# A graph network of four residual layers on one core: three tiles of source rows fetched by one-hot products instead of indirect DMA

## What is computed

```python
# layer 2 (src, dst and etypes have 400,000 entries)
h_src = feat[src]
for r in range(16):
    mask = etypes == r
    msg = msg + h_src * mask[:, None].astype(feat.dtype) @ weight[r]
out = jax.ops.segment_sum(msg, dst, num_segments=feat.shape[0])
# layer 3
m = jnp.concatenate([x[row], x[col], edge_attr], axis=1)
h = jnp.maximum(m @ W1 + b1, 0.0)
h = jnp.maximum(h @ W2 + b2, 0.0)
h = h @ W3 + b3
s = jax.ops.segment_sum(h, col, num_segments=n)
agg_max = jax.ops.segment_max(h, col, num_segments=n)
o = jnp.concatenate([x, agg_mean, agg_max, u[batch]], axis=1)
```

## Time and profile before

| | us |
|---|---|
| median of 3 runs | 12724.05 |
| lowest, highest | 12720.05, 12810.73 |
| the profiled execution's own time | 12744.54 |
| its span | 12742.7 |

### The profile page before, as it was taken

The page is one execution under the profiler, slowest core; times in us unless marked ns, Lnnn a source line. Parts: engine busy times, 40 slices in busy tenths (PEclk is TensorE's granted clock), DMA queues, the critical chain, the costliest instruction groups (busy, mean ns, idle before and its releaser), DMA issues. The chain is left out here.

```text
span 12742.7 us, 117881 instructions
## 1 busy us (share of the span) xinstructions
PE 2970.5 (23%) x12074; PEld 2055.6 (16%) x12074; DVE 6179.3 (48%) x21579; ACT 1252.9 (10%) x3613; POOL 9537.5 (75%) x9956
## 2 busy tenths in 40 slices
PE   2000011111100640000000000013545545545455
PEld 2000011111100320000000000012333333333334
DVE  8877477777743432222222222224555555555555
ACT  3111111111111330000000000000101001011001
POOL 7777777777777767777777777777777777777776
PEclk6555555555555775555555555555555555555556
DMA  6444444444444432222222222222222222222221
GB/s 168 120 118 116 115 127 117 118 116 118 116 119 115 127 120 74 66 66 74 66 70 66 66 66 72 68 52 55 68 67 67 67 68 67 67 67 67 67 67 49
DMA packets 766546, 1107.81 MB, mean 87 GB/s; under 512 B 277264, under 2 KB 383263, under 8 KB 765038
## 3 DMA queue, kind: packets, MB, share of 16 engines
q0 software_dynamic: 328208, 302.76, 12.8%
q1 hardware_dynamic: 257781, 569.91, 12.3%
q10 hardware_dynamic: 179944, 229.99, 6.1%
HBM read 548.77 MB, written 553.01 MB: 86 GB/s over the span
## 5 line engine op out<-in xcount | busy, mean ns | idle before, releaser
L137 POOL DMA_INDIRECT g<-in_edge_attr,idxs x3072 | 2955.4, 962 | 938.3 <-issue 857.1
L137 POOL DMA_INDIRECT yg<-ytab,idx x3077 | 2911.6, 946 | 949.4 <-issue 920.1
L137 POOL DMA_INDIRECT msg<-Y,idx x3025 | 2874.0, 950 | 984.8 <-issue 923.5
L1600 DVE SCALAR_TENSOR_TENSOR run<-run,same,msg 128x64 f32<-128x64 f32 x3125 | 891.0, 285 | 2910.9 <-DMA msg<-Y,idx 2803.4
L611 DVE SCALAR_TENSOR_TENSOR run<-run,sameD 128x80 f32<-128x80 f32 x3072 | 907.9, 296 | 1324.3 <-DMA g<-in_edge_attr,idxs 882.5
L2023 DVE SCALAR_TENSOR_TENSOR run<-run,same,ps 128x32 f32<-128x32 f32 x3125 | 774.7, 248 | 1584.1 <-PE ps L1917 1428.7
L1156 PE MATMUL ps<-tail,before 128*128 128x64 f32 (+2 forms) x10 | 2.8, 421 | 4456.5 <-PEq L1470 3811.3
L1901 PE MATMUL ps<-ident,zx 128*128 128x128 f32 x1564 | 524.8, 439 | 1460.6 <-DMA yg<-ytab,idx 1430.5
L2006 DVE SCALAR_TENSOR_TENSOR zx<-zx,same,zs 128x32 f32<-128x32 f32 x3124 | 793.4, 254 | 135.3 <-DVE anew L1989 28.6
L615 DVE SCALAR_TENSOR_TENSOR runS<-runS,sameS,g 128x64 f32<-128x64 f32 x3072 | 852.4, 277 | 0.1
L1000 PE MATMUL ps<-hot 128*98 128x128 bf16 x3072 | 373.1, 315 | 1816.3 <-DVE hot L718 1816.3
(11 more groups left out here) (356 smaller groups left out, 5893.0 us busy)
## 6 DMA issues: line engine op xcount, KB each, us to landing
R<-run SPq DMA_DIRECT2D x390, 320.0 KB, 2.3
msg<-Y ACTq DMA_DIRECT2D x6400, 0.2 KB
msg<-Y SPq DMA_DIRECT2D x6400, 0.2 KB
R<-run SPq DMA_DIRECT2D x195, 512.0 KB, 3.0
R<-run SPq DMA_DIRECT2D x124, 800.0 KB, 5.3
v<-in_edge_attr ACTq DMA_DIRECT2D x384, 256.0 KB
yg<-ytab SPq DMA_DIRECT2D x6144, 0.1 KB
RA<-runS SPq DMA_DIRECT2D x256, 256.0 KB, 2.9
```

The lines of the kernel that those rows point to most:

```text
L137: eng.indirect_dma_start(out=out, out_offset=None, in_=table, in_offset=bass.IndirectOffsetOnAxis(ap=index, axis=0)).then_inc(sem, 16)
L1600: ins_ = v.scalar_tensor_tensor(out=run[:, q, t, :], in0=prev, scalar=same[:, q, t:t + 1], in1=msg[:, q, t, :], op0=ALU.mult, op1=ALU.add)
```

## The change

In `edges_2`, tiles 6 and 18 of all 125 slots are no longer gathered. x, which lies in SBUF as 98 rows of 64 values per partition (node p * 98 + b), is kept as three bf16 parts whose sum is exact. For a tile, a node's index is split into a key, index // 7, and a rest. PE spreads the key over the partitions (`spread_key`), DVE compares it with 14 places (`one_hots`: 14 x 128 values a tile), PE multiplies the 14 one-hots by the three parts (`find`), DVE picks one of 7 rows by a mask (`pick`), PE turns the rows (`turn`), DVE copies them (`keep_turned`), PE multiplies them by the 16 matrices (`relate`), and DVE picks one of 16 by a mask (`pick_rel`). These steps run one to three slots ahead. In `edges_3`, tile 4 of the 192 whole slots is taken from `ytab`, loaded once into SBUF, by `spread_key`, `one_hots`, `find` and `pick`, two to four slots ahead; the PSUM area of `turn` becomes single. POOL makes two small index ramps in each stage. Two sets of semaphores are now made in the build function.

```diff
+HOT2 = (6, 18)
+HOTS = len(HOT2)
+HN, HB2 = 14, 7
+HOT3 = 4
...
@@ edges_2, POOL @@
-                    if t == ROW_AT2 and q in BY_ROW:
+                    if t in HOT2 or t == ROW_AT2 and q in BY_ROW:
...
@@ edges_2, PE @@
+            def spread_key(c, q):
+                pe.wait_ge(keyed, NS2 * c + q + 1)
+                for u in range(HOTS):
+                    last = nc.tensor.matmul(psK[:, u * P:(u + 1) * P], key[:, u:u + 1].to_broadcast([P, P]), k.ident[:, :],
+                                            start=True, stop=True)
+                last.then_inc(key_spread, 1)
+            def find(c, q):
+                for u in range(HOTS):
+                    pe.wait_ge(hot_ready, HOTS * (NS2 * c + q) + u + 1)
+                    for i in range(HN):
+                        for part in parts_x:
+                            last = nc.tensor.matmul(psX[:, u, :], hot[:, u, i, :], part[:, i * HB2 * D:(i + 1) * HB2 * D],
+                                                    start=i == 0 and part is parts_x[0], stop=i == HN - 1 and part is parts_x[2])
+                last.then_inc(x_found, 1)
+            def turn(c, q):
+                hold(pe, x_ready, NS2 * c + q + 1, k.passed)
+                for u in range(HOTS):
+                    last = nc.tensor.transpose(psT[:, u * P:(u + 1) * P], rows_x[:, u, :], k.ident[:, :])
+                last.then_inc(x_turned, 1)
+            def relate(c, q):
+                pe.wait_ge(xT_ready, NS2 * c + q + 1)
+                for u in range(HOTS):
+                    for a in range(0, RELS * D, 512):
+                        last = nc.tensor.matmul(psW[:, u * RELS * D + a:u * RELS * D + a + 512], rows_xT[:, u * P:(u + 1) * P],
+                                                W[:, a:a + 512], start=True, stop=True)
+                last.then_inc(rels_made, 1)
+            def slot(c, q):
+                for work, m in ((turn, 1), (find, 2), (spread_key, 3), (relate, 1)):
+                    if within(*after(c, q, m)):
+                        work(*after(c, q, m))
...
@@ edges_2, DVE @@
+            def one_hots(c, q):
+                v.wait_ge(key_spread, NS2 * c + q + 1)
+                for u in range(HOTS):
+                    v.tensor_tensor(hot[:, u], over(psK[:, u * P:(u + 1) * P], 1, HN), over(place[:, :], 2, P),
+                                    ALU.is_equal).then_inc(hot_ready, 1)
+            def pick(c, q):
...
+                v.wait_ge(x_found, NS2 * c + q + 1)
+                s.link(v.tensor_tensor(picked[:, :, :, :], psX.rearrange("p u (b f) -> p u b f", f=D), over(mask[:, :, :], 3, D),
+                                       ALU.mult))
+                v.tensor_reduce(rows_x[:, :, :], picked[:, :, :, :].rearrange("p u b f -> p u f b"), AX.X, ALU.add)\
+                    .then_inc(x_ready, 1)
+            def keep_turned(c, q):
+                v.wait_ge(x_turned, NS2 * c + q + 1)
+                v.tensor_copy(rows_xT[:, :], psT).then_inc(xT_ready, 1)
+            def pick_rel(c, q):
+                v.wait_ge(rels_made, NS2 * c + q + 1)
+                for u in range(HOTS):
+                    s.link(v.tensor_tensor(by_rel[:, :, :], psW[:, u * RELS * D:(u + 1) * RELS * D].rearrange("p (r f) -> p r f", f=D),
+                                           over(rmask[:, u, :], 2, D), ALU.mult))
+                    s.link(v.tensor_reduce(msg[:, q, HOT2[u], :], by_rel[:, :, :].rearrange("p r f -> p f r"), AX.X, ALU.add))
+            def ahead(c, q):
+                pick_rel(c, q)
+                for work, m in ((pick, 1), (one_hots, 2), (next_key, 3)):
+                    if within(*after(c, q, m)):
+                        work(*after(c, q, m))
             def slot(c, q, part):
+                ahead(c, q)
+                scan(c, q, part)
+                if within(*after(c, q, 1)):
+                    keep_turned(*after(c, q, 1))
...
@@ edges_3, PE @@
-                if behind:
-                    pe.wait_ge(turned_c, n + 1 - LANES)
+                if lags(c, q, 1):
+                    pe.wait_ge(turned_c, n)
...
             def body(c):
                 for q in range(NS3):
                     slot(c, q, SL3)
-
-            turns(pe, CHUNKS3, body)
+                    for work, m in ((find, 2), (spread_key, 4)):
+                        if within(*after(c, q, m)):
+                            work(*after(c, q, m))
...
@@ edges_3, DVE, body after aggregate and meta @@
+                    for work, m in ((pick, 2), (one_hots, 3), (next_key, 4)):
+                        if within(*after(c, q, m)):
+                            work(*after(c, q, m))
```

More of the change, by code:

```diff
@@ L1503, in row_tile, with after, within @@
             list_rows(eng, c + 1, q)
+        def after(c, q, m):
+            return c + (q + m) // NS2, (q + m) % NS2
+        def within(c, q):
+            return not (isinstance(c, int) and c >= CHUNKS2)
         def last_slot(c, q):
@@ L1572, in _ @@
             body(LAST)
+        @block.tensor
+        def _(pe):
+            W = k.W2r[0:D, :, :].rearrange("i r o -> i (r o)")
+            def spread_key(c, q):
[28 more added lines that the diff above has]
+                        work(*after(c, q, m))
+            spread_key(0, 0)
+            pe.wait_ge(parts_done, 1)
+            find(0, 0)
+            spread_key(0, 1)
+            turn(0, 0)
+            find(0, 1)
+            spread_key(0, 2)
+            relate(0, 0)
+            for q in range(NS2):
+                slot(0, q)
+            with pe.Fori(1, LAST) as c:
+                for q in range(NS2):
+                    slot(c, q)
+            for q in range(NS2):
+                slot(LAST, q)
@@ L1576, in _, with next_key @@
             s = Steps(v, vsteps)
-            s.link(v.memset(run[:, NS2 - 1, SL2 - 1, :], 0.0))
-            def slot(c, q, part):
+            def next_key(c, q):
+                copy_at(v, key[:, :], hot_key[:, bass.ds(NS2 * c + q, 1), :].rearrange("p a u -> p (a u)")).then_inc(keyed, 1)
+            def one_hots(c, q):
[3 more added lines that the diff above has]
+                                    ALU.is_equal).then_inc(hot_ready, 1)
@@ L1584, in slot @@
                         if last_slot(c, q):
-                            v.wait_ge(late[t // part], 16 * (part - (t // part == ROW_AT2 // part)))
+                            fetched = [i for i in range(t, t + part) if i not in HOT2 and i != ROW_AT2]
+                            v.wait_ge(late[t // part], 16 * len(fetched))
                             if t // part == ROW_AT2 // part:
@@ L1607, in slot @@
                         s.done(ins_)
+            prepare()
+            s.link(v.memset(run[:, NS2 - 1, SL2 - 1, :], 0.0))
             s.fresh()
@@ L1809, in ps, with after, within @@
         def ps(stage, q):
-            return k.ps[:, LANES * stage + q % LANES, 0:W]
+            return k.ps[:, LANES * stage + (q % LANES if stage else 0), 0:W]
+        def after(c, q, m):
+            return c + (q + m) // NS3, (q + m) % NS3
+        def within(c, q):
+            return not (isinstance(c, int) and c >= CHUNKS3)
         def groups(steps):
@@ L1919, in slot, with spread_key, find @@
                 last.then_inc(fin, 1)
+            def spread_key(c, q):
+                pe.wait_ge(keyed, NS3 * c + q + 1)
+                nc.tensor.matmul(psK, key[:, 0:1].to_broadcast([P, P]), k.ident[:, :], start=True, stop=True)\
+                    .then_inc(key_spread, 1)
+            def find(c, q):
+                pe.wait_ge(hot_ready, NS3 * c + q + 1)
+                for i in range(HN):
+                    for part in parts_y:
+                        last = nc.tensor.matmul(psP, hot[:, i, :], part[:, i * HB2 * MSG:(i + 1) * HB2 * MSG],
+                                                start=i == 0 and part is parts_y[0], stop=i == HN - 1 and part is parts_y[2])
+                last.then_inc(y_found, 1)
             def body(c):
@@ L2030, in aggregate, with next_key, one_hots, pick @@
                         b.then_inc(run_ready, 1)
+            def next_key(c, q):
+                copy_at(v, key[:, :], hot_key[:, bass.ds(NS3 * c + q, 1)]).then_inc(keyed, 1)
+            def one_hots(c, q):
+                v.wait_ge(key_spread, NS3 * c + q + 1)
+                v.tensor_tensor(hot[:, :, :], over(psK, 1, HN), over(place[:, :], 2, P), ALU.is_equal).then_inc(hot_ready, 1)
+            def pick(c, q):
+                s.done(v.tensor_tensor(mask[:, :], seq[:, :], hot_in[:, bass.ds(NS3 * c + q, 1)].to_broadcast([P, HB2]), ALU.is_equal))
+                v.wait_ge(y_found, NS3 * c + q + 1)
+                s.wait(s.n)
+                s.link(v.tensor_tensor(picked[:, :, :], psP.rearrange("p (b f) -> p b f", f=MSG), over(mask[:, :], 2, MSG), ALU.mult))
+                v.tensor_reduce(yg[:, q, HOT3 * MSG:(HOT3 + 1) * MSG], picked[:, :, :].rearrange("p b f -> p f b"), AX.X, ALU.add)\
+                    .then_inc(y_picked, 1)
@@ L2043, in _ @@
             spread_z(0, 0, SL3)
```

(8 more changed lines are left out.)

117 lines of the change are left out of this document (111 added, 6 removed).

## The result

| | before | after |
|---|---|---|
| median, us | 12722.05 | 13644.6 |
| lowest, highest | 12718.79, 12810.73 | 13642.55, 13650.13 |
| the profiled execution's own time | 12744.54 | 13643.6 |
| its span | 12742.7 | 13641.9 |

The changed kernel is slower: the ratio is 1.0708, with an interval of 1.0661 to 1.0754. The forecast was 13640 us. Ratios compare only executions in the faster of the two states that a program can be in, while the medians are over all of them. The spans differ by 899.2 us. The difference divides at the starts and ends of the two stages, read as the first and last starts of the two scan lines as in the earlier trace rows: the last scan operation of the relational stage starts at 8935.3, not 8439.0 (+496); the third stage then starts another 25 later (9268.5 against 8747.6) and its last operation stands at 13479.0, not 12582.4, another +376.

The account below looks back on a forecast made before the run. POOL's gather queue was taken to bound both stages; new PE-DVE chains of 32.4 and 23.0 us a slot add +292 and +623, total +915 on 12744.5: 13660, 20 lower for the median, 13640 us; range 13,150 to 14,300.

Parts of the forecast that it names:

- POOL bound before, not after: Both stages: POOL's gather queue set 30.3 and 19.7 us slots; afterwards its waits are no longer issue.
- 2.4 tiles: Both stages: wording for the POOL time saved per slot, leaving 27.9 and 18.5 us a slot.
- 2.5 gathers: Relational stage: wording for the saving per slot if POOL still set the pace, -311 us in all.
- The closed chain of the relational stage: Relational stage: pick_rel, pick, first one-hot, find, key, relate in sequence set the slot at 32.4 us; +292 us.
- strided reductions cost double: Rival, DVE's pick_rel and pick: strided views add 3.4 us, third-stage pick 0.2; about 14,100 us, chance 0.10.
- reductions over 1.3 us: DVE's reductions: durations above this were named as a sign that the forecast was wrong.
- The new wait of the third stage: Third stage: PE's key product waits 3 us or more for DVE's next key; slots 23 us apart, +623 us.
- The level of the clock there: Third stage, PE: 24.5 us at 1.2 GHz, 22.7 with two groups at the upper level; 23.0 taken.
- Stays up: Rival, PE's clock: grant holds while DVE has its turn; +15 - 55, about 12,690 us, chance 0.08.
- Never rises in find: Rival, PE's clock: mostly zero one-hots keep it low, slots 49.5 and 24.5 us; about 16,060 us, chance 0.07.
- Closer products: Rival, find: 448 columns under 0.16 us, so POOL sets the relational stage again; 13,040 us, chance 0.05.
- POOL goes on setting both stages, 12,190 us: Rival, both stages: removed gathers pay in full, -311 - 226; needs at most 27.9 and 18.5 us slots; chance 0.04.

Follow-up runs that it names:

- relate_early2: Changed kernel with relate ahead of find in PE's queue, keep_turned and pick_rel moved with it in DVE's (relational stage): 12972.15 us, ratio 1.0211 to before.
- key_mid2: Changed kernel with the third stage's spread_key moved from the slot's end to behind the gathered products: 13011.55 us, ratio 1.0221 to before.
- both_fill: Changed kernel with relate, keep_turned, pick_rel and third-stage spread_key reordered, plus 24 idle PE products behind the relational spread_key: 12202.99 us, ratio 0.9586 to before.
- both2: Changed kernel with relate, keep_turned and pick_rel reordered in the relational stage and spread_key moved in the third: 12371.79 us, ratio 0.973 to before.

## Why the forecast came out

The mechanism of the forecast was right, and two of its terms were wrong by some 200 us each, in opposite directions. The sum for the profiled execution was 13660 and came to 13643.6; the 20 us that the forecast took off for the median did not come, as the median is 1 us above the profiled execution. So the nearness to 5 us is luck; the sign and the rough size are not.

- **POOL bound before, not after.** Right. Its gaps were nearly all issue and now are ACT's index copies as well, which was named as the sign. In two places of the prediction's text ("2.4 tiles", "2.5 gathers") microseconds are called tiles and gathers: what is gone is two gathers of 24.2 in the one stage and one in the other, and the sums go by that.
- **The closed chain of the relational stage.** Right, in order and in closing, and `relate_early2` shows it: with all work kept, taking pick_rel (6.4 us) and the first one-hot (2.07) out from between two finds brings the slot from 34.0 to 28.5, although relate is up to 3.5 us slower there.
- **Its terms.** Find: 13 slow products, then 71 from 6216.4 to 6229.9 (0.19 us each), 18.3 us to the key's start; forecast 12 slow and 18.3. Key and relate took 4.3 us together, forecast 4.0. First one-hot 2.07 us, forecast 2.1. Pick 3.1 us, forecast 3.0, but by two errors: its reduction took 1.66 us, not 1.09, and masks and register addresses 0.35, not 0.7. **The term that was mis-sized is pick_rel**: 6.4 us, not 5.0. Its reductions take 1.87 us each and not the 1.21 of the earlier trace rows, which were over neighbouring values. The rival "strided reductions cost double" was half true: the factor is 1.5, in both lines, some 1.9 us a slot and not 3.4, and "reductions over 1.3 us", which the prediction had named as a sign of being wrong, is what came. From one pick_rel to the next the mean is 34.13 us in place of 32.4: over 123 turns +213. The chain starts at 4698.1, 12 us earlier than forecast, and its tail is 3 us longer, so the stage ended 204 us later than forecast (+496 against +292).
- **The new wait of the third stage.** Right: DVE's half of the chain was 10.65 us with the hand-over (forecast 11.0 without it), PE's 11.7 in the slot that is shown (forecast 11.7 with the two upper groups at 2.4 GHz). The start was 25 us later, forecast 26. `key_mid2` shows that the chain goes through the key: 21.78 to 18.34 with the key alone moved.
- **The level of the clock there was the mis-sized term.** I took 23.0, above the 22.7 of the working, to allow for slots whose upper groups run at 1.2 GHz. The slots went to the other side: the mean granted clock in the stage is 0.78, in the second slot shown the products are at their upper pace inside the gathered ones already, and the mean of the 188 turns is 21.97, which is 194 us less than forecast. The last slots got back 49 us, not 23. The forecast was +623 with start and tail, measured is +400.
- **The clock's two rivals.** "Stays up" did not come about: the first 13 products of each find are slow. "Never rises in find" neither: the one-hot products were at the upper level after 13 steps and 4.9 us, the dense ones of the earlier trace rows after 11 and 4.7 us.
- **Closer products.** The rival had under 0.16 us for 448 columns; measured is 0.19. The Trainium skill, "TensorE: Matmul & The Clock Gate", section "Back-to-back issue gap", gives about 131 ns for 512 columns in such streams. The trace does not agree: the 71 products behind the slow lead stand 0.19 us apart at 448 columns, in finds that are all 18.2 to 18.6 us long.
- **POOL goes on setting both stages, 12,190 us.** Wrong for this order of the queues. But in `both_fill` POOL sets both stages, which is its condition, and the kernel came to 12,203. So the price of the removed gathers was about right as well (forecast -311 and -226; measured -297 at the end of the relational stage, -236 behind it). The order of the queues in the diff cost 1314.6 us of span, the distance to `both2`: the 899.2 that were lost and 415.4 that were not gained.

The condition that was given there was too narrow. It asked for the upper clock throughout and a few us less besides, as if the chain's order were given. What is in the chain is a choice of the two written programs, and I priced only the one in the diff.

## What to carry to other kernels

Where two engines hand over to each other in order, write down the closed chain of a slot (who waits for whom until the same operation of the next slot) and compare it with the old bound before adding work, however low the busy shares are: here they were 0% and 24%, and the new work still took over. Then look for links that the longest block need not wait for, here pick_rel ahead of find, and for a block in the queue whose input comes late, here the key, and move them before asking for less work. A reduction over a view with a large step took 1.5 times one over neighbours here, and changing which side has the step won nothing.

## What was unexpected of the hardware

- An f32 DVE operation with a step of 28, 64 or 256 bytes on one side takes 1.52 to 1.61 times as long in SBUF for 896 or 1024 values, read or written.
- PE's clock and its work are tied to each other: moving relate behind a wait of 2.5 us made it up to 7.2 us long where it had been 3.7, and 2.8 us a slot of useless products made the whole kernel 118 us faster in the profile.
- PE's clock fell within relate, in the middle of uninterrupted work, in the group of eight instructions that starts at 7007.91 above; the granted clock in two stretches of `both2` is 0.98 and then 0.50 while PE is busy throughout:

```profile
7007.90:7009.90 2.00, 1.99 (x5) 1.02 (x6) 2.00 (x2) 0.00 (x0) 1.53 (x2) 0.98 0.22 35
7009.90:7013.10 3.20, 3.20 (x4) 0.72 (x3) 3.06 (x7) 0.00 (x0) 2.28 (x3) 0.50 0.20 23
```

A level that falls behind the idle time, and not in it, was already in the earlier trace rows, where the grant was still 1.00 in an idle stretch. So in these rows what a product costs is set by what the engine did some time before it, and not only by what it does now.
